# The last step of a causal attention cut into two steps of 256 queries

## The reference

```python
x = x + s4(layernorm(x))            # gates i, f, o, s; scan over the tokens
x = x + ffn(layernorm(x))           # first feed-forward layer
x = x + attention(layernorm(x))     # 16 heads of 16 channels, causal, then Wo
x = x + ffn(layernorm(x))           # second feed-forward layer, same weights
# ffn(x): x_prev = x moved by one token
#   r = sigmoid((mu_r*x + (1-mu_r)*x_prev) @ W_r.T)
#   k = (mu_k*x + (1-mu_k)*x_prev) @ W_k.T
#   out = r * (relu(k)**2 @ W_v.T)
```

## Time and profile before

| | |
|---|---|
| median of 3 executions | 1856.88 us (1855.34 to 1861.38) |
| the profiled execution, its own time | 1857.59 us |
| its span in the profile | 1855.9 us |
| PE busy | 1749.0 us (94%) |
| DVE busy | 1583.7 us (85%) |
| ACT busy | 1312.5 us (71%) |
| POOL busy | 530.3 us (29%) |
| mean granted clock of PE | 0.985 of full speed |

### The profile page before, as it was taken

How to read it: one execution, slowest core, us unless ns; L and a number is a source line. 1 busy time by engine, 2 the same in 40 slices (tenths; PEclk the granted TensorE clock), 3 DMA queues, 4 the chain that set the end, 5 groups by cost and what they waited for, 6 DMA issues and landing times.

```text
span 1855.9 us, 34235 instructions
## 1 busy us (share of the span) xinstructions
PE 1749.0 (94%) x12684; PEld 755.4 (41%) x12684; DVE 1583.7 (85%) x3175; ACT 1312.5 (71%) x2757; POOL 530.3 (29%) x655
## 2 busy tenths in 40 slices
PE   6689999999999999999999999999999999999997
PEld 5565546354444343353443333433432233332224
DVE  4566789897989998999999999999999999999802
ACT  2235474647676877748778878788778888888893
POOL 5556645544432232432213022131110001110001
PEclk9988999999999999999999999999999999999998
DMA  3131202121020000020002000000110000000000
GB/s 105 40 63 33 50 19 49 38 41 34 16 51 12 20 15 23 12 46 12 28 17 34 6 1 17 28 1 6 33 25 5 6 4 3 13 1 7 1 1 12
DMA packets 56954, 42.99 MB, mean 23 GB/s; under 512 B 8788, under 2 KB 56788, under 8 KB 56788
## 3 DMA queue, kind: packets, MB, share of 16 engines
q1 hardware_dynamic: 53188, 39.74, 8.8%
q10 hardware_dynamic: 3600, 1.06, 0.4%
HBM read 24.00 MB, written 16.25 MB: 22 GB/s over the span
## 4 chain that ended last, share of the span: by engine, by line
PE 29%; DVE 22%; ACT 6%; POOL 3%; issue 2%; DVEq 0%; POOLq 0%; ACTq 0%
DVE span_max L1284 19%; PE psum L1531 9%; PE psum L1510 6%; PE psum L1478 5%; ACT probs L1069 5%; PE psum L1347 4%; PE psum L1341 3%; POOL rows L846 1%; PE psum L1335 1%; DVE rows L1252 1%; DVE small L1143 0%; POOL small L841 0%; PE psum L1540 0%; PE psum L1485 0%; POOL probs L953 0%
## 5 line engine op out<-in xcount | busy, mean ns | idle before, releaser
L1284 DVE TENSOR_REDUCE span_max<-psum 128x1 f32<-128x512 f32 (+3 forms) x2304 | 1312.7, 635 | 73.4 <-PE psum L1478 36.4
L1069 ACT ACTIVATE probs<-psum 128x512 f32<-128x512 f32 (+3 forms) x2304 | 1115.5, 596 | 204.1 <-PE psum L1510 200.8
L1531 PE MATMUL psum<-probs,v_aug 128*17 128x512 f32 (+3 forms) x4608 | 569.2, 566 | 5.8 <-POOL probs L953 4.3
L1478 PE MATMUL psum<-k_stack,q_stack 48*128 48x512 f16 (+3 forms) x2304 | 520.0, 364 | 15.5 <-DVE span_max L1284 8.9
L1510 PE MATMUL psum<-q_stack,k_stack 50*128 50x512 f16 (+3 forms) x2304 | 515.5, 367 | 6.5 <-ACT probs L1069 1.5
L1510 PEld LDWEIGHTS psum<-q_stack,k_stack 50*128 50x128 f16 x2304 | 137.5, 93 | 510.9 <-ACT probs L1069 440.4
L953 POOL TENSOR_SCALAR_AFFINE_SELECT probs<-probs 128x512 f32<-128x512 f32 x128 | 82.0, 643 | 603.0 <-ACT probs L1069 602.9
L1478 PEld LDWEIGHTS psum<-k_stack,q_stack 48*128 48x128 f16 x2304 | 165.1, 94 | 197.4 <-DVE span_max L1284 111.3
L846 POOL TENSOR_SCALAR rows<-rows,small 128x256 f32<-128x256 f32 x140 | 174.3, 1253 | 7.4
L1531 PEld LDWEIGHTS psum<-probs,v_aug 128*17 128x17 f32 x4608 | 76.6, 95 | 137.6 <-issue 112.7
L995 ACT ACTIVATE rows<-psum,cols 128x256 f32<-128x256 f32 x128 | 53.6, 470 | 83.7 <-PE psum L1341 83.2
(11 more groups left out here) (118 smaller groups left out, 1347.7 us busy)
## 6 DMA issues: line engine op xcount, KB each, us to landing
q_stack<-q_parts SPq DMA_DIRECT2D x192, 32.0 KB, 2.0
k_stack<-k_parts SPq DMA_DIRECT2D x42, 128.0 KB, 4.8
rows<-in_x SPq DMA_DIRECT2D x16, 256.0 KB, 3.0
q_parts<-rows SPq DMA_DIRECT2D x32, 128.0 KB, 1.9
k_parts<-rows SPq DMA_DIRECT2D x32, 128.0 KB, 2.0
out<-rows SPq DMA_DIRECT2D x16, 256.0 KB, 2.2
x_rows<-rows SPq DMA_DIRECT2D x14, 256.0 KB, 2.1
rows<-x_rows SPq DMA_DIRECT2D x14, 256.0 KB, 2.8
```

The lines of the kernel that those rows point to most:

```text
L1069: act.activation(probs[:, tile % PROBS, i, q0:], bank(b)[:, q0:], ACT.Exp, scale=SCALE / QK_SCALE).then_inc(exp_done, 1)
L1284: nc.vector.tensor_reduce(span_max[:, s % SPAN_RING, row:row + 1, k0 // SPAN:k0 // SPAN + 1], bank(b)[:, 0:k1 - k0], AX.X, ALU.max).then_i ...
L1478: ins = nc.tensor.matmul(bank(b)[:, 0:k1 - k0], q_stack[row:row + SCORE_ROWS, s % Q_RING, u, qt * P:(qt + 1) * P], k_stack[row:row + SCORE ...
L1531: ins = nc.tensor.matmul(pv_bank[32 * h:32 * h + VW, q0:], v_aug[:, j, g * HG + h, :], probs[:, tile % PROBS, h, q0:], start=(j == 0), sto ...
```

## The change

A step becomes (g, c, a, b): the queries from tile a to tile b of the chunk, in units of 128. All steps are (g, c, 0, 4) as before but the last one, (3, 7), which becomes step 31 = (3, 7, 0, 2) and step 32 = (3, 7, 2, 4). Each has its own DMAs of queries, its own shift rows, sums and division. The maxima are the same instructions as before; step 31 has those of its 256 queries, step 32 the others. Step 31 has 30 tiles of keys and step 32 has 32; they are 256 queries wide but for one of 128 at the end of each. `aT` of unit 14 waits for the `norm` of step 31, that of unit 15 for the `norm` of step 32.

```diff
-STEPS = [(g, c) for c in range(CHUNKS) for g in range(GROUPS)]
-TILES = [(s, j) for s, (g, c) in enumerate(STEPS) for j in range(TT * (c + 1))]
+SPLIT = 1
+STEPS = [(g, c, a, b) for c in range(CHUNKS) for g in range(GROUPS)
+         for a, b in (((0, TT),) if c < CHUNKS - 1 or g < GROUPS - SPLIT else ((0, UT), (UT, TT)))]
+TILES = [(s, j) for s, (g, c, a, b) in enumerate(STEPS) for j in range(TT * c + b)]
+COMPLETES = [max(s for s, (g, c, a, b) in enumerate(STEPS) if c == u // 2 and a <= u % 2 * UT < b)
+             for u in range(UNITS)]
+def columns_of(tile):
+    s, j = TILES[tile]
+    g, c, a, b = STEPS[s]
+    return max(a, j - c * TT) * P, b * P
...
-        op(("aT", u), ("norm", (u // 2 + 1) * GROUPS - 1), ...
+        op(("aT", u), ("norm", COMPLETES[u]), ...
...
-                    act.activation(probs[:, tile % PROBS, i, q0:], bank(b)[:, q0:], ACT.Exp,
+                    act.activation(probs[:, tile % PROBS, i, q0:q1], bank(b)[:, q0:q1], ACT.Exp,
...
-                    act.activation(oT[:], pv_bank, ACT.Copy).then_inc(o_copied, 1)
+                    cut = slice(STEPS[s][2] * P, STEPS[s][3] * P)
+                    act.activation(oT[:, cut], pv_bank[:, cut], ACT.Copy).then_inc(o_copied, 1)
...
-                    nc.tensor.matmul(bank(b)[:, q0:], k_stack[row:row + STACK, g * PAIRS + u, j * P:(j + 1) * P],
-                                     q_stack[row:row + STACK, s % Q_RING, u, q0:], start=True, stop=True)\
+                    nc.tensor.matmul(bank(b)[:, q0:q1], k_stack[row:row + STACK, g * PAIRS + u, j * P:(j + 1) * P],
+                                     q_stack[row:row + STACK, s % Q_RING, u, q0:q1], start=True, stop=True)\
```

More of the change, by code:

```diff
@@ L196, in followed @@
         op(("x2+bo", u), ("load_x2", u) if u < UNITS - LATE else normalized(u, LN_A), ("bo.add",), ("x2+bo", u - 1))
-        op(("aT", u), ("norm", (u // 2 + 1) * GROUPS - 1), ("aT" if u == UNITS - 1 else "proj", u - 1, *([] if u == UNITS - 1 else [1])))
+        op(("aT", u), ("norm", COMPLETES[u]), ("aT" if u == UNITS - 1 else "proj", u - 1, *([] if u == UNITS - 1 else [1])))
         op(("aT.copy", u), ("aT", u))
@@ L235, in followed @@
         op(("oT", s), ("all pv", s), ("out", s - 1))
-        op(("out", s), ("oT", s), *[("aT", 2 * c - n) for n in (1, 2) if g == 0])
+        op(("out", s), ("oT", s), *[("aT", 2 * c - n) for n in (1, 2) if g == a == 0])
         op(("recip", s), ("out", s))
@@ L298, in due @@
         later = covered[MAXIMA_UPTO[min(s + 1, len(STEPS) - 1)]]
-        return upto + (later - upto) * (j + 1) / (TT * (STEPS[s][1] + 1)) + AHEAD
+        return upto + (later - upto) * (j + 1) / (LAST_TILE[s] - LAST_TILE.get(s - 1, -1)) + AHEAD
     def may_begin(u):
         s, j = TILES[min(scored, len(TILES) - 1)]
-        g, c = STEPS[s]
-        part = (g + (j + 1) / (TT * (c + 1))) / GROUPS
+        g, c, a, b = STEPS[s]
+        part = (g + (j + 1) / (TT * c + b)) / GROUPS
         return u < 2 * UT or c + part + LEAD + 1 >= u // 2 + (u % 2) * 0.5
@@ L320, in width @@
     def width(tile):
-        s, j = TILES[tile]
-        return CHUNK - max(0, j - STEPS[s][1] * TT) * P
+        a, b = columns_of(tile)
+        return b - a
     def bank_for(kind, t):
@@ L352, in ready_pv @@
         s, j = TILES[tile]
-        on_diagonal = j >= STEPS[s][1] * TT
-        if on_diagonal and tile not in mask_seen or not j and s and ("oT", s - 1) not in seen:
+        if on_diagonal(tile) and tile not in mask_seen or not j and s and ("oT", s - 1) not in seen:
             return never
-        at = mask_seen[tile] if on_diagonal else exp_seen[tile]
+        at = mask_seen[tile] if on_diagonal(tile) else exp_seen[tile]
         return max(at, seen["oT", s - 1]) if j == 0 and s else at
@@ L1058, in _ @@
                     base = SHIFT_BASE * (s % 2)
-                    act.activation(shift_rows[base:base + HG * MAX_ROWS], bank(BANK["shift", s])[0:HG * MAX_ROWS],
-                                   ACT.Copy).then_inc(shift_copied, 1)
+                    cut = slice(STEPS[s][2] * P, STEPS[s][3] * P)
+                    act.activation(shift_rows[base:base + HG * MAX_ROWS, cut],
+                                   bank(BANK["shift", s])[0:HG * MAX_ROWS, cut], ACT.Copy).then_inc(shift_copied, 1)
                 elif op[0] == "exp":
@@ L1464, in _ @@
                     s, qt, u, k0, k1 = MAXIMA[m]
-                    g, c = STEPS[s]
+                    g, c, first, upto = STEPS[s]
                     maxed += 1
@@ L1491, in _ @@
                     pe.wait_ge(shift_ready, s + 1)
-                    for qt in range(TT):
+                    for qt in range(*STEPS[s][2:]):
                         ins = nc.tensor.matmul(
@@ L1500, in _ @@
                     s, j = TILES[tile]
-                    g, c = STEPS[s]
-                    q0 = max(0, j - c * TT) * P
+                    g, c, first, upto = STEPS[s]
+                    q0, q1 = columns_of(tile)
                     row, u = HALF * (i % 2), i // 2
@@ L1515, in _ @@
                     s, j = TILES[tile]
-                    g, c = STEPS[s]
+                    g, c, first, upto = STEPS[s]
                     d = j - c * TT
-                    if d >= 0:
-                        pe.wait_ge(masked, s * TT + d + 1)
+                    if on_diagonal(tile):
+                        pe.wait_ge(masked, MASKS_UPTO[s] - upto + d + 1)
                     else:
```

60 lines of the change are left out of this document (35 added, 25 removed).

## The result

The changed kernel takes 1867.13 us in the median (8 executions, 1864.3 to 1869.57), the kernel before 1857.78 (8, 1854.84 to 1862.4). The ratio is 1.0046, with a 95% interval of 1.0032 to 1.006: some 8.5 us slower, where 6.4 were forecast. The time itself lies inside the stated range of 1857.5 to 1870, but above the 1860.5 to 1866 that I gave my own sum of 1863.3. The profiled execution has a span of 1864.6 us, 8.7 more than before.

What follows compares the result with a forecast made beforehand. DVE's maxima were taken to set the pace earlier, ACT's exponentials in the last step, and a chain of waits in the tail. Six terms sum to +6.4 us on 1856.9, giving 1863.3 us, range 1857.5 to 1870.

Steps and rivals of the forecast that it cites:

- 1, 2 and 4, the split: Last step split: narrower exponentials +7.7 us, idle ACT filled between steps 30 and 31 -0.9, waits between 31 and 32 +0.6.
- Term 1: Steps 31 and 32 on ACT: 248 narrower exponentials for 128, at 0.063 us fixed cost per instruction, +7.7 us.
- 3, DVE: Step 31's `neg`, `part0` and `part1` stand among the maxima while DVE bounds: +0.7 us, bounds 0.3 to 1.2.
- 5, unit 14: Unit 14's work inside step 32 holds up the exponentials on PE and ACT: +6.5 us, bounds 3.4 to 8.6.
- The walk tile by tile: Step 32: stalls of 1.5 us at `proj`, 1.7 at `k`/`r`, 1.2 at `kv`, with the ACT work some 6.9.
- 6, the tail: From the last exponential to the end, with one unit: 26.3 us against 34.5, -8.2 us, bounds -9.3 to -7.3.
- `proj` to `x3`: In the tail: 2.94 us for 12 matrix instructions before, 2.1 for 8 with one unit.
- Rival A: Not slower: a narrow tile costs PE 0.70 us, not 0.85, so unit 14's work adds 2.7; 1859.5 us, chance 0.27.
- B: Slower: ACT isn't full at 256 wide, idle 0.1 us per tile, 62 times, +6.2; 1869.5 us, chance 0.15.
- C: PE's clock halves in the narrow steps, over a third of the 62 tiles, +12 us; 1875 us, chance 0.05.

Runs made afterwards that it cites:

- e1: The changed kernel's split alone, with unit 14 also waiting for step 32; ratio to the kernel before 1.0034.
- e7: The changed kernel with one exponential for two heads in steps 31 and 32, 124 instructions in place of 248; 1859.13 us, ratio to the kernel before 1.0003.
- e3: The changed kernel with unit 14's `proj`, `k`, `r` and `kv` jobs kept apart on PE; ratio to the kernel before 1.0049.
- e4: The changed kernel with unit 14's `k`, `r` and `kv` placed behind unit 15's `proj`; ratio to the kernel before 0.9999.
- e6: The changed kernel with 18 products that nobody reads in PE's waits behind the last exponential; 1860.91 us, ratio to the kernel before 1.0015.
- e9: The changed kernel with the last two steps split and maxima of the last four narrow steps allowed three steps ahead; 1875.7 us, ratio to the kernel before 1.01.

## Why the prediction was right, and where its sizes were off

The mechanism held: a shorter tail, paid for twice on the engine that bounds. The sizes held less well, and I had given no more than even odds to a loss of over 0.3%. By its own terms:

- **1, 2 and 4, the split** (+7.7, -0.9, +0.6 = +7.4). e1's head gives +7.5. The stalls at the two borders were 0.57 and 0.25 us, for 0.6 and 0.3. Term 1 by itself is borne out by e7: pairing takes 6.8 off the head, 7.8 less what PE gives back. By the Trainium skill's figures (ScalarE: Activation LUTs, What ACT_TABLE_LOAD costs), 186 ns less an overlap of about 93, a narrow exponential would take an estimated 0.31 us and the term would be 11.2; the trace does not agree, at 0.27 us in the row of 116.
- **3, DVE** (+0.7). Nothing in the head. The cost was there: `neg`, `part0` and `part1` of step 31 stand among the maxima of step 30, and DVE comes to its next `neg` 1753.35-1700.47 = 52.88 us behind the common row, 52.35 before, 0.53 later. But it was not on the path: from the common row to the group at 1750.71 the exponentials take 50.11 us before, and 50.05 in the changed kernel (rows below). The step that failed is that whatever delays DVE there delays the exponentials. With PE at 97% in the same row I should have asked which of the two they wait for; no run tried it by itself.

ACT's timeline of the kernel before:

```profile
1700.60 2.06 ACT L1069 ACTIVATE probs<-psum 128x512 f32<-128x512 f32 x4 [0.31 <-PE psum L1510]
...
1750.71 4.90 ACT L1069 ACTIVATE probs<-psum 128x512 f32<-128x512 f32 x10 [0.31 <-PE psum L1510]
```

DVE's, in the same kernel:

```profile
1752.95 0.28 DVE L1290 TENSOR_REDUCE neg_max<-span_max 128x16 f32<-128x128 f32 x1
```

And ACT's and DVE's of the changed kernel:

```profile
1750.52 2.07 ACT L1089 ACTIVATE probs<-psum 128x512 f32<-128x512 f32 x4 [0.31 <-PE psum L1536]
...
1753.35 0.22 DVE L1312 TENSOR_REDUCE neg_max<-span_max 128x8 f32<-128x64 f32 x1
```

- **5, unit 14** (+6.5). 7.7, inside the bounds of 3.4 to 8.6. The walk tile by tile had the stalls right: 1.5 at `proj`, 1.7 at `k`/`r` and 1.2 at `kv`, and ACT's idle time there is 1.4, 1.5 and 1.5, 4.4 in either sum. What was too small is the rest. Unit 14's instructions on ACT take 2.7 us from start to start (0.48 at 1798.69, 0.53 at 1807.33, 1.65 at 1813.39), not 2.5. Each of the six stalls costs some 0.1 more than the idle time in its row (1.94 where 1.11+0.73 = 1.84), some 0.6 in all. And I took 6.5 where the walk gave 6.9, without a reason. 4.4+2.7+0.6 = 7.7. The 3.4 us of PE's slack in the lower bound hardly counted: a lone job of 1.06 us costs 1.94-1.11 = 0.83, so that only the slack of its own tile, 0.23, pays for it. That the other tiles' slack can't be saved up, since PE doesn't run ahead of a ring of three tiles and five banks, is argued from the code; e3, which spreads the jobs and gains nothing, agrees. e4 divides the term: `aT`, `proj` and `ffnT` cost 130.8-128.2 = 2.6, `k`, `r` and `kv` 5.1.
- **6, the tail** (-8.2). -6.3. The step that failed is `proj` to `x3`, "for 8 it is 2.1", which came to 3.9 (1841.13 to 1844.99): I left the clock as before up to the statistics. It fell ahead of `aT` instead, and `proj` and `aT` paid 1.8+0.5, while `k` to the last `kv` took 1858.51-1852.29 = 6.2, 0.3 under my 6.5. e6 confirms the price of the clock: filled, the same `proj` and `aT` take 1.98 and 0.64. Why it fell there is open. That PE has less to do ahead of `aT` than before doesn't explain it, for e1 gives it the same instructions between the last exponential and `aT`, 1.44 of 2.89 us for 1.45 of 2.90, and kept its full clock until behind `ffnT`. The stretch in e1, then in the changed kernel:

```profile
1828.29:1831.18 2.89, 1.44 (x19) 0.48 (x19) 0.50 (x2) 0.38 (x1) 0.64 (x1) 1.00 0.00 0
```

```profile
1836.37:1839.27 2.90, 1.45 (x19) 0.50 (x19) 0.50 (x2) 0.39 (x2) 0.64 (x1) 0.98 0.00 0
```

- The sum: 7.4+0+7.7-6.3 = 8.8 against 8.7 measured in the span. The two errors that count, 1.2 and 1.9, went the same way, and term 3's 0.7 the other; that it took something off them was luck. The time of 1867.13 is 3.8 over my 1863.3: 2.9 in the difference of the medians (9.35 for 6.4), 0.9 since the kernel before stood at 1857.78, not 1856.9.

Rival A (cheap narrow tiles) falls with the 4.4 us of idle time and with e3; a narrow tile took PE 0.56+0.32 = 0.88 us, not 0.70. B falls with the gapless 116 exponentials. C: in the narrow steps the clock stayed at its upper level, as this stretch of step 31 shows:

```profile
1761.00:1790.00 29.00, 28.70 (x314) 10.04 (x313) 0.68 (x2) 28.81 (x104) 0.00 (x0) 1.00 0.01 2
```

PE counts as busy for 28.7 of 29 us there, although its loads wait for ACT in nearly every tile; where a matrix instruction ends is modelled in the profile, so that such short waits don't show in the share. The Trainium skill (TensorE: Matmul & The Clock Gate, A second HAM failure mode: psum-queue depth-cycling) has the clock swing with frequent short idling and cycling banks; that doesn't show in these two steps. In one other kernel with narrow steps, e9, the clock did fall once, at the border between two of them:

```profile
1769.80:1773.20 3.40, 3.40 (x29) 0.69 (x31) 0.50 (x2) 2.14 (x8) 0.00 (x0) 0.53 0.00 0
```

There ACT waited 0.96 us for the scores, so that rival C is excluded for the changed kernel and not for every kernel of this kind. That the clock would go where PE has real pauses, in the tail, I had noted and priced too low.

## What to carry to other kernels

Cutting the last piece of a pipeline to start its successor sooner was paid for here by fixed costs per instruction on the engine that bounds, and by the successor's work, which moves from a stretch with slack into one without; ask of each moved operation whether its old place was free. Where only part of a successor lies on the path, move its chain forward and leave its bulk behind, in the waits of the piece that ends last (e4), and keep the columns of an instruction whole when the piece is cut (e7). When a row shows one engine at 99% and another at 97%, it doesn't say which of them a delay or a saving will reach (term 3, and e9, where the halts of DVE went and the time stayed); try it before pricing it.

## What the runs showed of the hardware

- Putting more work on PE made the tail shorter. Six jobs more took it from 28.2 to 24.1 us, and products that nobody reads from 34.5 to 31.2 and from 28.2 to 23.6. The row at half clock had PE busy for 9.83 of 17 us. Each of these tails is that of one profiled execution; the ratios go the same way.
- Where the clock falls differs between kernels that are nearly alike in the tail, one execution each: ahead of `aT` in the changed kernel for 17 us, behind `proj` in the kernel before for 10, and behind `ffnT` in e1 for 7. What PE does between the last exponential and `aT` is the same in the changed kernel and in e1 (1.45 of 2.90 us, 1.44 of 2.89), so that this alone doesn't decide it.
- An exponential over two heads of 256 columns, which lie 1024 elements apart in `probs`, costs what one of 512 adjoining columns does: 0.48 us in a row of 56, against 0.49.
